# A graph attention layer on one core: three row tiles' sums to a PSUM bank, an earlier first product, and half of V made by GpSimd

## The reference, cut to what matters

```
h = relu(layernorm(x))                      # x: 4096 x 128
h = h @ W.T + b_W                           # 4096 x 128
e = (h @ a1)[:, None] + (h @ a2)[None, :] + b_a
e = where(e > 0, e, 0.2 * e)
attention = softmax(where(adj > 0, e, -9e15), axis=1)     # adj: 4096 x 4096 int32
out = x + attention @ h
```

## Time and profile before

| | us |
|---|---|
| median of 3 runs | 221.06 (219.03 to 222.19) |
| the profiled execution | 220.54 |
| its span, first to last instruction | 219.0 |
| outside the span | 1.54 |
| mean granted TensorE clock | 0.984 |
| PE busy | 202.3 (92%) |
| DVE busy | 184.0 (84%) |
| ACT busy | 159.0 (73%) |
| POOL busy | 26.2 (12%) |

### The profile page before, as it was taken

One profiled execution on the slowest core, in us unless ns is written; L12 is line 12 of the kernel. 1 busy time (PEld: TensorE's weight loads), 2 busy tenths in 40 slices (PEclk: granted clock), 3 DMA queues, 4 the chain that ended last, 5 costly groups with the idle time before them and its releaser, 6 DMA issues.

```text
span 219.0 us, 7197 instructions
## 1 busy us (share of the span) xinstructions
PE 202.3 (92%) x3176; PEld 195.7 (89%) x3176; DVE 184.0 (84%) x265; ACT 159.0 (73%) x166; POOL 26.2 (12%) x55
## 2 busy tenths in 40 slices
PE   0993986989999999999999999999999999999993
PEld 0671975889999999999999999999999999999993
DVE  3872373699999979999997899999979799999743
ACT  2375599999999737778965787789666877896300
POOL 1099990000000000007000000000000000000000
PEclk9999699699999999999999999999999999999999
DMA  6899948889999999999999999999999999999011
GB/s 180 313 406 408 403 147 294 295 290 344 356 315 401 428 406 406 408 405 407 405 287 418 409 408 407 413 403 409 349 416 411 405 408 413 403 406 325 15 51 48
DMA packets 24192, 75.66 MB, mean 346 GB/s; under 512 B 1632, under 2 KB 5984, under 8 KB 24032
## 3 DMA queue, kind: packets, MB, share of 16 engines
q1 hardware_dynamic: 24016, 75.06, 89.6%
q10 hardware_dynamic: 144, 0.13, 0.3%
HBM read 73.08 MB, written 2.11 MB: 343 GB/s over the span
## 4 chain that ended last, share of the span: by engine, by line
issue 60%; ACT 9%; DMA 8%; DVE 7%; PE 2%; POOL 2%; SPq 1%; POOLq 0%; ACTq 0%; DVEq 0%
DVE w L459 6%; DMA g_row<-g_dram 5%; ACT mask L376 5%; DMA g_dram<-gT 3%; PE ps L776 2%; ACT fin L362 2%; ACT H L319 1%; SPq L295 1%; POOL bad L697 1%; POOL tt L696 1%; POOL bad L698 0%; ACT hT L313 0%; ACT g_row L328 0%; POOL tt L695 0%; PE ps L721 0%
## 5 line engine op out<-in xcount | busy, mean ns | idle before, releaser
L733 PE MATMUL ps<-V,w 128*128 128x129 f16 x1024 | 179.2, 221 | 3.5 <-ACT g_row L328 2.3
L735 PE MATMUL ps<-V,w 128*128 128x129 f16 x1024 | 179.1, 224 | 0.0
L739 PE MATMUL ps<-V,w 128*128 128x129 f16 x1024 | 179.1, 220 | 0.0
L459 DVE SCALAR_TENSOR_TENSOR w<-g_row,pairs,mask 128x1024 f32<-128x1024 f32 x124 | 151.6, 1280 | 10.3 <-ACT mask L376 6.6
L376 ACT ACTIVATE mask<-adj_sb 128x2048 bf16<-128x2048 int32 x64 | 121.6, 1907 | 32.1 <-DMA adj_sb<-in_adj_t 32.1
L733 PEld LDWEIGHTS ps<-V,w 128*128 128x128 f16 x1024 | 99.8, 97 | 4.5 <-ACT g_row L328 2.4
L739 PEld LDWEIGHTS ps<-V,w 128*128 128x128 f16 x1024 | 102.6, 100 | 0.0
L735 PEld LDWEIGHTS ps<-V,w 128*128 128x128 f16 x1024 | 100.6, 98 | 0.0
L702 POOL PARTITION_ALL_REDUCE bad<-bad x1 | 0.4, 380 | 113.4 <-DVE bad L498 113.4
L721 PEld LDWEIGHTS ps<-wp,hT 128*128 128x128 f32 x64 | 9.3, 211 | 4.4 <-issue 2.9
L668 POOL TENSOR_TENSOR x_sb<-x_sb,b_row 128x256 f32<-128x256 f32 x16 | 11.1, 728 | 9.4 <-issue 9.4
(11 more groups left out here) (85 smaller groups left out, 63.6 us busy)
## 6 DMA issues: line engine op xcount, KB each, us to landing
adj_sb<-in_adj_t SPq DMA_DIRECT2D x64, 1024.0 KB, 8.3
xT<-in_x_t SPq DMA_DIRECT2D x8, 256.0 KB, 7.3
out<-xT SPq DMA_DIRECT2D x7, 256.0 KB, 4.2
x_sb<-in_x_p SPq DMA_DIRECT2D x3, 512.0 KB, 7.7
g_row<-g_dram SPq DMA_DIRECT2D x1, 1536.0 KB, 11.3
x_sb<-in_x_p SPq DMA_DIRECT2D x2, 256.0 KB, 4.1
wp<-in_w_pack ACTq DMA_DIRECT2D x1, 131.0 KB, 4.0
out<-xT SPq DMA_DIRECT2D x1, 128.0 KB, 2.0
```

Of the source, the lines that this page charges most:

```text
L459: nc.vector.scalar_tensor_tensor(w[:, m % SLOTS, side * GC:(side + 1) * GC], g_ps if m < FROM_PS else g_row[:, group * GC:(group + 1) * GC ...
L733: nc.tensor.matmul(ps[:, k, 0:NF], w16[:, m % SLOTS, col:col + P, 1], V[:, jt, 0:NF], start=(jt == 0), stop=False, skip_group_check=True)
L735: nc.tensor.matmul(ps[:, k, 0:NF], w16[:, m % SLOTS, col:col + P, 1], V[:, jt, NF:2 * NF], start=False, stop=False, skip_group_check=True)
L739: last = nc.tensor.matmul(ps[:, k, 0:NF], w16[:, m % SLOTS, col:col + P, 0], V[:, jt, 0:NF], start=False, stop=(jt == NT - 1), skip_group_ ...
```

## The change

- **PSUM.** Three row tiles' sums share a bank (129 columns each), so a group needs three banks. Groups 0 and 2 use banks 0 to 2, group 1 uses banks 3 to 5, group 3 takes banks 3 to 7 with its last three tiles in a bank each. Chunks of h from c = 3 on and the centred chunks go through banks 3 to 5. The spread row stays in banks 6 and 7 for the whole of group 0 (L452 reads it there for steps 0 to 15), and the copy to `g_row` is gone.
- **Order on PE.** Step 0 is issued after `h_chunk(4)` and `centre_chunk(5)`; the last h chunks stand between steps 0, 1, 2 and 3.
- **Order of the loads.** The first four adjacency loads go between the loads of x. There are 5 buffers.
- **ACT.** The masks of steps 0 and 1 go to DVE (`early_mask`, L460). The exponentials come in three parts (8, 8 and 16 tiles) instead of two. `products` and `highs` remain for chunks 0 and 1 alone.
- **GpSimd.** For chunks 2 to 7 it makes the whole of V (`halves`, L713 to L715): two multiplications and a subtraction over 4 x 129 elements. Adding b_W to x is moved behind that, in larger instructions.
- **Ends of groups.** `take_sums` is gone; ACT scales a group's sums straight from the PSUM, once for each group.
- **Stores.** One store for each of groups 0 to 2, later in the queue; `PIECES` are now of 3, 2, 1, 1 and 1 tiles.

```diff
-    HELD = 4
+    HELD = 5
-    PARTS = ((0, GI), (GI, NT))
+    PARTS = ((0, GI), (GI, 2 * GI), (2 * GI, NT))
-    PIECES = ((0, 4), (4, 6), (6, 7), (7, 8))
+    PIECES = ((0, 3), (3, 5), (5, 6), (6, 7), (7, 8))
+    X_BANK = (0, 3, 0, 3, 3, 3, 3, 3)
+    H_BANK = (1, 4, 1, 4, 4, 4, 4, 4)
+    def sums_at(group, k):
+        if group < NG - 1:
+            return 3 * (group % 2) + k // 3, k % 3
+        return ((3, 0), (3, 1), (3, 2), (4, 0), (4, 1), (5, 0), (6, 0), (7, 0))[k]
...
+                def early_mask(m):
+                    dve.wait_ge(adj_loaded[m % HELD], 16 * (m // HELD + 1))
+                    nc.vector.tensor_scalar(mask[:, m % MASKS, :], adj_sb[:, m % HELD, :], CONNECTED, 0.0, ALU.mult,
+                                            ALU.max).then_inc(mask_early, 1)
...
-                                                   g_ps if m < FROM_PS else g_row[:, group * GC:(group + 1) * GC],
+                                                   g_ps if group == 0 else g_row[:, (group - 1) * GC:group * GC],
...
+                def halves(c):
+                    r = slice(c * CT, (c + 1) * CT)
+                    part = 1 if c < 4 else 2
+                    pool.wait_ge(scaled_ready, part + 1)
+                    pool.wait_ge(ones_ready, part + 1)
+                    pool.wait_ge(h_ready, c + 1)
...
+                    nc.gpsimd.tensor_tensor(V[:, r, 0:NF], H[:, r, H0:HC], by, ALU.mult)
+                    step(nc.gpsimd.tensor_tensor(prod[:, c % 2, :, :], H[:, r, H0:HC], by, ALU.mult))
+                    nc.gpsimd.tensor_tensor(V[:, r, NF:2 * NF], prod[:, c % 2, :, :], V[:, r, 0:NF],
+                                            ALU.subtract).then_inc(v_ready, 1)
...
+                deviations(2)
+                deviations(3)
+                halves(2)
+                deviations(4)
+                halves(3)
+                add_b(0)
+                add_b(1)
+                for c in range(4, NCH):
+                    halves(c)
...
+                whole(0)
+                h_chunk(5)
+                centre_chunk(6)
+                whole(1)
+                h_chunk(6)
+                centre_chunk(7)
+                whole(2)
+                h_chunk(7)
+                for m in range(3, NM - ENDS):
```

More of the change, by code:

```diff
@@ L96, in gat_layer_kernel @@
         w = sb("w", [P, SLOTS, 2 * GC], F32)
-        g_row = sb("g_row", [P, N], F32)
+        g_row = sb("g_row", [P, N - GC], F32)
         V = sb("V", [P, NT, 2 * NF], F16)
@@ L377, in mask_part, with scale_rows @@
                                          scale=CONNECTED).then_inc(mask_ready, 1)
[L379 to L382 removed]
+                def scale_rows(group):
+                    act.wait_ge(rg_ready, group + 1)
+                    for k in range(GI):
                         g = GI * group + k
[L384 to L396 removed]
+                        bank, a = sums_at(group, k)
+                        ins = nc.scalar.activation(Z[:, g, :], sums[:, bank, a, 0:DOUT], ACT.Copy, scale=rg[:, g:g + 1])
+                        if k % 4 == 3:
+                            ins.then_inc(scaled_rows, 1)
                 act.dma_start(wp[:], w_pack).then_inc(wp_loaded, 16)
@@ L594, in _ @@
                 statistics(2)
-                statistics(3)
                 scores(0)
@@ L607, in _ @@
                 nc.vector.tensor_scalar(tt[:, 5:6], tx[:, 0:1], -SLOPE, SHIFT, ALU.mult, ALU.add).then_inc(shift_ready, 1)
-                statistics(4, 3, 6)
+                early_mask(0)
                 pack(0)
                 scale_weights(0)
-                statistics(4, 6, 8)
+                scores(1)
+                statistics(3)
                 dve.wait_ge(pairs_ready, 1)
@@ L614, in _ @@
                 weigh(0, 0)
+                lows(0)
                 weigh(0, 1)
-                lows(0)
-                weigh(1, 0)
-                weigh(1, 1)
-                scores(1)
-                lows(1)
+                early_mask(1)
                 pack(1)
                 scale_weights(1)
+                weigh(1, 0)
+                lows(1)
+                weigh(1, 1)
                 dve.wait_ge(pairs_ready, 2)
+                statistics(4)
+                weigh(2, 0)
+                weigh(2, 1)
+                weigh(3, 0)
+                weigh(3, 1)
+                scores(2)
+                weigh(4, 0)
+                weigh(4, 1)
+                pack(2)
+                scale_weights(2)
+                dve.wait_ge(pairs_ready, 3)
                 nc.vector.transpose(gT[:], pairs[:, 0, :]).then_inc(gT_ready, 1)
-                dve.wait_ge(g_row_ready, 2)
-                for m in range(FROM_PS, NM):
+                for m in range(5, NM):
                     group, at = divmod(m, PAIRS)
@@ L720, in h_chunk @@
                         tile = (c % 2) * CT + j
-                        last = nc.tensor.matmul(ps[:, 2 + 2 * (c % 2) + j // 2, at:at + 2 + DOUT],
+                        last = nc.tensor.matmul(ps[:, H_BANK[c] + j // 2, at:at + 2 + DOUT],
                                                 hT[:, tile * P:(tile + 1) * P], wp[:, WA:WA + 2 + DOUT], start=(j % 2 == 0),
@@ new lines, in _ @@
+                h_chunk(0)
+                pe.wait_ge(norm_ready, 1)
+                centre_chunk(2)
+                h_chunk(1)
+                centre_chunk(3)
+                h_chunk(2)
+                pe.wait_ge(t_limits, 1)
+                nc.tensor.matmul(ps[:, G_BANK + 1, 0:P], tt[:, 0:1].to_broadcast([P, P]), ident[:],
+                                 start=True, stop=True).then_inc(t_spread, 1)
+                h_chunk(3)
+                centre_chunk(4)
+                pe.wait_ge(t_bounds, 1)
@@ new lines, in _ @@
+                pe.wait_ge(pairs_ready, 1)
+                for k in range(2):
+                    for j in range(CT):
+                        last = nc.tensor.matmul(ps[:, G_BANK + k, j * P:(j + 1) * P],
+                                                pairs[:, 0, k * CT + j:k * CT + j + 1].to_broadcast([P, P]),
+                                                ident[:], start=(j == 0), stop=(j == CT - 1), skip_group_check=True)
+                    last.then_inc(rows_spread, 1)
+                h_chunk(4)
@@ L818, in gat_layer_kernel @@
+                for i, (k0, k1) in enumerate(PIECES):
+                    for m in range(NM - ENDS, NM):
+                        ins = products(m, k0, k1)
+                        if i == len(PIECES) - 1:
+                            ins.then_inc(mm_done, 1)
+                    if i < len(PIECES) - 1:
+                        ins.then_inc(acc_done, 1)
         with nc.Block() as block:
```

327 lines of the change are left out of this document (140 added, 187 removed).

## The result

The changed kernel takes **209.41 us** (median of 4 runs, 208.89 to 209.82). The kernel before, measured beside it, took 221.2 (4 runs, 219.03 to 222.19), so the ratio is **0.948, with a 95% interval from 0.9405 to 0.9552**: 5.2% faster. The profiled execution took 209.82, with a span of 208.2 against the 211.5 of my sum: 3.3 us to explain. Its mean granted clock was 1.00.

A forecast was written before the change was run, and what follows sets the result against it. PE was taken to set the end once it runs: step 5 at 44.2 us instead of 51.7 cuts the span from 219.0 to 211.5, plus 1.54 outside it gives 213.0 us; range 210.0 to 219.5.

The forecast's parts named there:

- my sum: Whole kernel: PE starts step 5 at 44.2 us instead of 51.7, so the span falls from 219.0 to 211.5 us.
- the start of step 5: PE's stream: from this step it never waits again; 42.5 us, or 44.2 with the clock term, against 51.7 before.
- DVE's mask: Early chain, twice on the path: a 128x2048 mask on DVE takes 1.2 us, with 2.3 as upper bound.
- The third packing: Sign on DVE ahead of step 5: its rows keep the earlier spacing of 0.2 us, and not 1.4.
- Rivals 1 and 3: Early chain: masks at 2.3 us plus lower clock, 217.4, chance 0.13; GpSimd slower and the bound, 226.3 us, chance 0.10.
- GpSimd's V: V's chunks on GpSimd: 1.40 to 1.45 us a row, 4.3 us a chunk, hidden with 4.4 us cover.
- I add 1.7 for one such stretch: Early chain on PE: short gaps bring one stretch at the lower clock, adding 1.7 us before step 5.
- Rival 5: PE: no stretch at the lower clock, and shorter steps; 209.5 to 211.3 us, chance 0.06.
- x's fourth set: Early loads: complete at 19.9 us; its DVE statistics take 1.65 us, to 21.6, before the first weights.
- Rival 2: DVE rows before step 5 wait for GpSimd instructions to end; 5.6 us more, 218.6 us, chance 0.13.
- ACT waiting for its mask buffers rather than for DMA after 100 us: Sign in the changed profile: after 100 us ACT's waits are for its mask buffers, no longer for DMA.
- The DMA's cover: End of the run: loads end at 188 us, the last adjacency is needed by 195.4, leaving 7.4 us.

The follow-up runs named there:

- masks on ACT: Changed kernel with the masks of steps 0 and 1 made by ACT again instead of DVE; 210.31 us, ratio 0.9486.
- V on ACT and DVE: Changed kernel with V's chunks 2 to 7 made by ACT and DVE again, none by GpSimd; 214.82 us, ratio 0.9723.
- GpSimd under the packing: Changed kernel with four of GpSimd's additions of b ahead of V's chunk 4 instead of two; 212.68 us, ratio 0.960.
- loads of before: Changed kernel with the first adjacency load behind x's sets again, the others after it; 211.18 us, ratio 0.9516.
- chunks first: Changed kernel with the last h and centred chunks ahead of step 0 on PE again, ACT's order kept; 215.43 us, ratio 0.9735.
- gap on purpose: Changed kernel with the statistics of x's fourth set moved ahead of the first packing on DVE; 213.21 us, ratio 0.9646.
- counterpart: V on ACT and DVE, with GpSimd's additions of b only after step 11; 210.86 us, ratio 0.9537.

## Why the prediction was right, and where it was wrong

**What held.** Counting by the start of step 5, and the flow from there: 163.1 us of products and 3.8 of tail, as in the sum. DVE's mask at 1.22 us, where I had taken 1.2 of 1.2 to 2.3. The Trainium skill, VectorE: DVE Perf Modes, section "The perf-mode tier table (the rule you actually need)", has 1227 ns for 2048 fp32 elements of such an instruction; the two rows of 1.22 agree, for int32 to bf16. The third packing at 0.2 us a row, no idle PE after 50 us, the last adjacency in by 189.8 (I asked for before 196; the sum had it at 188), the weights from the PSUM at 1.28 each. Rivals 1 and 3 did not come: no mask at 2.3, and GpSimd's V, far from slow, is done with chunk 4 at 43.2 where step 8 needs it at 49.6.

**What failed is a term of 1.7 us, "I add 1.7 for one such stretch"**, that of the row's passes at the lower clock. There was none: they took 2.02 us at a granted clock of 1.00. Rival 5, "No stretch at the lower clock, and shorter steps", with a chance of 0.06, is what came, and the median lies 0.1 us under even its lower end.

The step behind the term was wrong by its own rows, in two ways. The stretches that I took it from follow gaps of 3.79 and 2.25 us, and my own chain had gaps of 0.7 and 1.6 there. And the sum had the row done at 20.1 while DVE wanted it only at 21.6, behind the statistics of x's fourth set: 1.7 us more for the row would have moved step 0 by 0.1 to 0.2 us there, not by 1.7. The runs put the gaps in a row; each is PE's idle time by its timeline and the granted clock of what follows:

| PE idle, us | kernel | clock then |
|---|---|---|
| 0.81 | changed kernel, ahead of the row | 1.00 |
| 1.70 | masks on ACT | 1.00 |
| 2.25 | before, step 2 | 0.57 at 39 |
| 2.27 | V on ACT and DVE, step 4 | 0.68 in 40 to 45 |
| 2.35 | GpSimd under the packing, step 5 | 0.77 in 45 to 50 |
| 2.56 | loads of before | 0.50 |
| 2.57 | chunks first | 0.50 |
| 3.25 | gap on purpose | 0.50 |
| 3.79 | before, ahead of the row | 0.54 |

Where the stretch came at the row it cost 1.1 us and not 1.7 (loads of before, gap on purpose); behind the waits before steps 4 and 5 it cost 1.5, and with the chunks first about 2.4. The gap on purpose shows it with one edit, though that edit also makes the gap, and the two are told apart only by the durations of PE's rows.

The table is no rule. It has one execution of each kernel, and the unprofiled ones differ: the loads of before have the lower level in two executions of four. The idle time alone does not decide it either: the 4.3 to 5.1 us in which PE waits for its first load, in every run, are followed by a clock of 1.00.

**Mis-sized by 1.2 us: when PE starts step 5** (42.5 in the sum, 41.28 in the trace). I had x's fourth set in at 19.9; it is there at 17.55 in the kernel that waits for it. Two parts make up the 2.4 us. From 5 to 10 us the queue carries 347 GB/s, not 285 as before (the stretch above), 0.31 MB more, 0.76 us at 0.41 MB a us. And the adjacency that I reckoned from landed behind 4.9 MB by my count, but by the stretches 5.9 MB had been moved at 18.8; in the changed kernel 5.7 had at 17.55, against 5.4 by count. That fits transfers that overlap, so that a mark taken from a landing has part of the next ones in it (no run shows this by itself): 1.0 MB there, 0.3 here, and the 0.7 between them are 1.6 us. With the set in, DVE goes straight from the first packing to its statistics, and the first weights start at 20.24, not 21.6.

The rest is 0.4 from the count back from PE's end: the sum has 163.5 us from step 5 to the last product (51.7 to 215.2), and they took 163.1. 1.7, 1.2 and 0.4 are the 3.3 us of the span. Against the median the miss is 3.6.

**GpSimd's V was priced at 1.40 to 1.45 us a row and takes 1.05, 1.05 and 1.14.** It cost nothing here, being covered either way, except that the small DVE row at 36.07 took 0.5 us longer beside it. What moving V there is worth came out at 1.7 us by the counterpart, not the 3.6 of `lows` on DVE.

**Rival 2 has the right mechanism and the wrong chance of being hit.** I argued against it with L548, two SBUF operands in 0.18 us under GpSimd's L686. The large rows speak otherwise: 1.14 to 1.20 instead of 0.18 in two kernels, one of which only moves 1.25 us instructions of GpSimd under the packing. The Trainium skill, SBUF — State Buffer, section "Who interferes with whom", says that the shared port pair is an exclusive lock for the length of an instruction; the trace agrees for GpSimd rows of 516 and 512 columns, and does not show it for L686. With the loads of before, DVE's two-operand L566 (22.77 to 23.46) lies wholly inside L686 (22.04 to 23.71), and both have their usual length, 0.69 and 1.67 us. What I had not seen is that the 5.6 us, the middle of 0 and 11.2, supposed GpSimd busy under all of the packing; it was idle there, by 0.07 us, which I had not worked out: luck. The price when hit is 2.0 us for the packing and 1.5 for the clock, 3.5 and not 5.6.

**"ACT waiting for its mask buffers rather than for DMA after 100 us" did not come**: it waits 31.5 us for DMA over the run, before 32.1, with masks every 2.55 us (the one at 100.68 and the next at 103.20), and 5.9 us for its buffers. With the paces of 2.55 for DMA and 2.77 for PE the lead grows by 0.2 us a step, so the buffers fill only slowly; neither wait costs anything. The DMA's cover was smaller than the 7.4 us of the sum: by the same count (8.0 us ahead of PE's last product at 204.4, less 2.4 and 1.9) the last adjacency had to land by 192.1 and did at 189.8, 2.3 us.

**Left open**: how much three sums to a bank brought by themselves. They are what lets the chunks and the sums stand side by side in the PSUM, and no kernel with the order and without them was tried. Nor was the PSUM row for steps 2 to 15 undone alone, or the store order; that PE's 2.25 us for the copy to `g_row`, and the clock of 0.57 and less behind them, are gone is seen in the two traces only. Undone one at a time, the masks are worth 1, the loads 1.8, V on GpSimd 1.7 and the order on PE 1.5 to 6.0 us. That is 6 to 10.5 of the 11.8 us, if they add up, which no run shows; the rest is not assigned.

## What to carry to other kernels

Date the stream by the step from which the bounding engine flows without a gap, and value a reordering by the idle time that it removes and not by how early the first product is: 7.2 us of an earlier first product were worth 1.5. Before you put a clock penalty into a sum, look up the gap that each known stretch followed, and compare it with the gap of your own chain. An instruction that moves to GpSimd brings its length into DVE's small rows when they meet, so check what GpSimd runs beside a chain of short DVE rows on the path, and by what margin it does not, not only whether GpSimd keeps up.
